# Turning the 128-row tiles by ScalarE copies and VectorE 32x32 block transposition instead of by TensorE, in a two-layer kernel on one core

## The reference, cut to what matters

```
# layer 0
y = conv1d(x, weight, groups=4, taps=9) + cond @ c_weight.T + bias      # (64, 64, 1024)
base = y @ base_w.T + base_b
top 2 of 16 experts by softmax(y @ router_w.T), combine weights
delta = sum_e combine[e] * (y @ A.T) @ B[e].T * 0.5                      # rank 64
x = x + base + delta
# layer 1
att = softmax(mlp(cond));  mixW = sum_k att[k] weight[k];  y = mixW @ x + att @ bias_k
top 2 of 28 experts by y @ gate_W.T
x = x + y @ base_W.T + sum_e gate[e] * 2 * (y @ lora_A[e].T) @ lora_B[e].T   # rank 8
```

## Time and profile before

| | |
|---|---|
| median of three runs | 1252.92 us (1252.64 to 1259.85) |
| the profiled execution | 1253.69 us |
| its span, first to last instruction | 1251.9 us |
| granted TensorE clock, mean | 0.997 |
| busy: TensorE, its weight loads | 1228.3 us (98%), 1093.2 us |
| busy: VectorE, ScalarE, GpSimd | 636.9, 376.2, 286.7 us |
| DMA | 266.94 MB, mean 213 GB/s |

### The profile page before, as it was taken

One profiled execution on the slowest core, in us unless ns is written; L12 is line 12 of the kernel. 1 busy time (PEld: TensorE's weight loads), 2 busy tenths in 40 slices (PEclk: granted clock), 3 DMA queues, 4 the chain that ended last, 5 costly groups with the idle time before them and its releaser, 6 DMA issues.

```text
span 1251.9 us, 21917 instructions
## 1 busy us (share of the span) xinstructions
PE 1228.3 (98%) x7263; PEld 1093.2 (87%) x7263; DVE 636.9 (51%) x1807; ACT 376.2 (30%) x801; POOL 286.7 (23%) x307
## 2 busy tenths in 40 slices
PE   6999989999999999999999999999999999999998
PEld 6999989999999999999888787887888888888887
DVE  6666466556555444547744343353345454354452
ACT  4312212212333334333343433434322212222221
POOL 2012543333222222225412121111121211211200
PEclk9999999999999999999999999999999999999999
DMA  7566656765899999988799999999864454445410
GB/s 285 186 221 222 229 189 224 246 229 211 240 298 292 309 308 296 320 279 215 178 246 283 281 267 288 283 274 285 247 140 118 98 118 116 92 118 110 103 50 34
DMA packets 85179, 266.94 MB, mean 213 GB/s; under 512 B 23457, under 2 KB 27937, under 8 KB 77858
## 3 DMA queue, kind: packets, MB, share of 16 engines
q1 hardware_dynamic: 72608, 230.12, 56.8%
q0 software_dynamic: 11264, 35.66, 16.1%
q10 hardware_dynamic: 1266, 0.70, 0.2%
HBM read 154.24 MB, written 112.20 MB: 213 GB/s over the span
## 4 chain that ended last, share of the span: by engine, by line
PE 85%; DMA 5%; DVE 3%; issue 2%; POOL 2%; SPq 2%; ACT 1%; ACTq 0%; POOLq 0%; DVEq 0%
PE z L1367 22%; PE z L1369 21%; PE z L1368 21%; DMA x8raw<-in_x_dram 3%; PE c L1367 3%; PE c L1369 3%; PE c L1368 3%; PE c L1432 2%; PE t L1488 2%; PE c L1434 2%; PE c L1436 2%; PE t L1408 2%; DMA x_dram<-xb 1%; SPq L434 1%; POOL hs_dram L665 1%
## 5 line engine op out<-in xcount | busy, mean ns | idle before, releaser
L1367 PE MATMUL z<-w_1h,yh 128*128 128x512 f32 (+1 forms) x504 | 187.4, 372 | 0.0
L1367 PE MATMUL z<-w_0h,yh 128*128 128x512 f32 (+1 forms) x504 | 186.0, 369 | 0.0
L987 DVE TENSOR_TENSOR yl<-t,yh 128x512 fp32r<-128x512 f32 x126 | 81.0, 685 | 205.6 <-ACT yh L743 205.5
L1369 PE MATMUL z<-w_1l,yh 128*128 128x512 f32 (+1 forms) x504 | 183.6, 364 | 0.0
L1369 PE MATMUL z<-w_0l,yh 128*128 128x512 f32 (+1 forms) x504 | 183.2, 364 | 0.0
L1368 PE MATMUL z<-w_1h,yl 128*128 128x512 f32 (+1 forms) x504 | 183.1, 363 | 0.0
L1368 PE MATMUL z<-w_0h,yl 128*128 128x512 f32 (+1 forms) x504 | 182.8, 363 | 0.0
L1367 PE MATMUL z<-w_2h,yh 128*128 128x252 f32 (+1 forms) x504 | 151.5, 301 | 8.6 <-DVE before L1045 5.0
L658 POOL TENSOR_TENSOR carrier<-ones_col 128x1 f32<-128x1 f32 x96 | 23.2, 242 | 576.7 <-DVE den L1054 139.3
L1369 PE MATMUL z<-w_2l,yh 128*128 128x252 f32 (+1 forms) x504 | 150.5, 299 | 0.0
L1368 PE MATMUL z<-w_2h,yl 128*128 128x252 f32 (+1 forms) x504 | 150.5, 299 | 0.0
(11 more groups left out here) (219 smaller groups left out, 2476.4 us busy)
## 6 DMA issues: line engine op xcount, KB each, us to landing
bd<-bd_dram SPq DMA_DIRECT2D x96, 512.0 KB, 6.6
zs_dram<-zt SPq DMA_DIRECT2D x96, 512.0 KB
hs_dram<-zt SPq DMA_DIRECT2D x34, 512.0 KB
x8raw<-in_x_dram SPq DMA_DIRECT2D x32, 516.0 KB
xin<-in_x_dram SPq DMA_DIRECT2D x32, 512.0 KB
x_dram<-xb SPq DMA_DIRECT2D x32, 512.0 KB, 7.8
out_dram<-xb SPq DMA_DIRECT2D x32, 512.0 KB, 2.9
bd_dram<-bd SPq DMA_DIRECT2D x8, 1024.0 KB
```

The lines of the kernel that those rows point to most:

```text
L987: V.tensor_tensor(o, v, y_places(s, high, b)[0], ALU.subtract).then_inc(s.y_lo[b], 1)
L1367: T.matmul(o, ah, wh, start=start, stop=False, **kw)
L1369: return T.matmul(o, ah, wl, start=False, stop=stop, **kw)
```

## The change: who turns the rows

For all tiles but tile 0 of layer 0 and tiles 0, 1 and 16 of layer 1 (there TensorE still turns), a tile is turned in two steps. `mid` holds the rows. ScalarE copies it to a new buffer `moved` in 16 copies of 32 partitions x 256 elements (`moves`, two parts of 8), each from one quadrant of 32 partitions to another, so that every 32x32 block already stands in the quadrant where it must end. Then VectorE transposes every 32x32 block within its quadrant, from `moved` back into `mid` (`turn_rows`: four instructions of 256 elements in layer 0, two of 512 in layer 1). `y_high` and `y_low` read `mid` in SBUF in place of `tp` in PSUM. The weights of layer 1 are laid out by the host in the matching order. There are two buffers `yh` now, but still one `yl`, so `y_low(t+1)` now waits for `base_done[1]` of tile t, in both layers.

The order moves with it. In layer 0, ScalarE does part 0 of the moves of tile t+1 ahead of the exponentials and part 1 behind `x8_high(t+2)` and `b_high`, ahead of `w1_high` and `y_high`; with lists, `outputs` 2 and 3 now come behind `y_high`. VectorE does `turn_rows` behind `x8_low`, `b_low`, `w1_low` and `listed_places`, then `y_low`, and `residual(1)` only behind that. TensorE's `conv(t+2)` now waits for the third output of the list step, and each `listed_pair(s, 0)` for the last output of the step before. In layer 1 `mixing(t+1)` comes right behind `over_y(2)`, the first listed pair behind `over_y(0)`, the second behind `over_y(1)`; ScalarE does `mixed_out`, the 16 copies, the outputs 0 and 1, `h1h`, then `x1_high(t+2)` (a tile earlier than before), `y_high`, outputs 2 and 3. Tiles 0 and 15 of layer 1 keep the old order (`late`). TensorE's loops now do two tiles per turn.

The core of the diff (helpers that only changed their arguments and the loop heads are left out):

```diff
-        yh = sb(ctx, "yh", [P, KC, P], F32R)
+        yh = [sb(ctx, f"yh{u}", [P, KC, P], F32R) for u in range(2)]
+        moved = sb(ctx, "moved", [P, L])
...
+        def turned_by_tensor(s, t):
+            return at(t, 0) or s is a1 and (at(t, 1) or at(t, NA))
+        def turned_rows(s, t, y, b):
+            if not turned_by_tensor(s, t):
+                return y[:, 4 * b:4 * b + 4, :], mid[:, HALF * b:HALF * (b + 1)].rearrange("p (k r) -> p k r", r=P)
...
+            def moves(s, t, part):
+                if part == 0:
+                    for b in range(2):
+                        act.wait_ge(s.c_out[b], t + 1)
+                    act.wait_ge(s.y_ps[1], t)
+                for q in (2 * part, 2 * part + 1):
+                    rows, w = slice(Q * q, Q * (q + 1)), slice(KC * Q * q, KC * Q * (q + 1))
+                    for i in range(P // Q):
+                        o = moved[Q * i:Q * (i + 1), w]
+                        if s is a0:
+                            mm = copy(o.rearrange("p (n m) -> p n m", m=Q),
+                                      mid[rows, :].rearrange("p (n m) -> p n m", m=NB)[:, :, Q * i:Q * (i + 1)])
+                        else:
+                            mm = copy(o, mid[rows, KC * Q * i:KC * Q * (i + 1)])
+                if part:
+                    mm.then_inc(moved_ready, 1)
...
+                if turned and not first:
+                    moves(a0, t + 1, 0)
                 exps(a0, t)
...
                 if exists(t + 2):
                     x8_high(t + 2)
...
+                if turned:
+                    moves(a0, t + 1, 1)
                 if w1_piece is not None:
                     w1_high(2, w1_pieces(2)[w1_piece:w1_piece + 1])
+                if turned:
+                    y_high(a0, t + 1, 1 - u)
                 if lists:
                     outputs(s, 2, cp, first=first_list)
                     outputs(s, 3, tp, first=first_list)
...
+            def turn_rows(s, tiles):
+                dve.wait_ge(moved_ready, tiles)
+                for b in range(2):
+                    if s is a0:
+                        for q in (2 * b, 2 * b + 1):
+                            w = slice(KC * Q * q, KC * Q * (q + 1))
+                            mm = V.transpose(mid[:, w].rearrange("p (j n c) -> p n j c", j=2, c=CI),
+                                             moved[:, w].rearrange("p (n j c) -> p n j c", j=2, c=CI))
+                    else:
+                        k = slice(4 * b, 4 * b + 4)
+                        mm = V.transpose(mid[:, :].rearrange("p (k q r) -> p q k r", k=KC, r=Q)[:, :, k, :],
+                                         moved[:, :].rearrange("p (q k c) -> p q k c", k=KC, c=Q)[:, :, k, :])
+                    mm.then_inc(s.y_ps[b], 1)
...
+                if exists(t + 1):
+                    turn_rows(a0, t + 1)
+                    dve.wait_ge(base_done[1], t + (0 if at(t, TILES - 2) else 1))
+                    y_low(a0, t + 1, 1 - u)
                 if not at(t, TILES - 2):
                     residual(i, u, 1)
-                if exists(t + 1):
-                    y_low(a0, t + 1)
...
-                    if lists:
-                        pe.wait_ge(zt_out, PER * s + 4)
-                    turn_conv(t + 1)
...
                 if exists(t + 2):
+                    if lists:
+                        pe.wait_ge(zt_out, PER * s + 3)
                     conv(t + 2)
...
+                if not late and not last:
+                    pe.wait_ge(zt_out, PER * s - 1 if lists else PER * WS if at(t, 1) else PER * WAVES * WS)
+                    mixing(t + 1)
...
+                    pe.wait_ge(a1.c_out[1], t + 2)
+                    pe.wait_ge(zt_out, PER * s)
+                    listed_pair(s, 0)
...
-        "w1": w1.reshape(KC, P, L + GC).transpose(1, 0, 2), "lb": lb.reshape(K1, 2, L),
+        "w1": w1.reshape(P // Q, KC, Q, L + GC).transpose(0, 2, 1, 3).reshape(P, KC, L + GC), "lb": lb.reshape(K1, 2, L),
```

More of the change, by code:

```diff
@@ L270, in build @@
         x1 = xin + [x1_2, x1_3]
+        listed += [zt[2][:, 2 * R0 * n:2 * R0 * (n + 1)].rearrange("p (k r) -> p k r", k=2) for n in range(HELD - 2)]
         id_zero, id_ready, iota_ready = sem("id_zero"), sem("id_ready"), sem("iota_ready")
@@ L384, in y_places @@
             return y[:, 4 * b:4 * b + 4, :], tp[b][:, :].rearrange("p (k r) -> p k r", r=P)
-        last_y = [bd[0][:, n, :].rearrange("p (k r) -> p k r", r=P) for n in range(2)]
-        def y_of(s, t):
-            return last_y if s is a0 and at(t, TILES - 1) else (yh, yl)
         def own_buffers(t):
@@ L856, in step0 @@
                     outputs(s, 1, tp, first=first_list)
+                if turned and first:
+                    moves(a0, t + 1, 0)
                 if exists(t + 2):
@@ L869, in step0 @@
                     outputs(s, 3, tp, first=first_list)
-                if exists(t + 1):
-                    for b in range(2):
-                        y_high(a0, t + 1, b)
                 if turn is not None:
@@ L905, in _, with next_rows, step1 @@
             y_high(a1, 0, 0)
-            y_high(a1, 0, 1)
             act.wait_ge(xb_ready, TILES)
-            def step1(i, v, first=False, last=False, lists=False, turn=None):
-                t = 4 * i + v
-                s = t - S1_LISTS + WS
+            def next_rows(t, i, v):
+                if t + 2 < TILES if isinstance(t, int) else True:
+                    act.wait_ge(a1.c_ps[1], t + 2)
+                    x1_high(t + 2, i + (v + 2) // 4, (v + 2) % 4)
+                    mix_high(t + 2)
+            def step1(i, v, first=False, last=False, late=False, before_late=False, lists=False, turn=None):
+                t, u = 4 * i + v, v % 2
+                s = t - S1_LISTS + WS
+                exps(a1, t)
+                if not last and not late:
+                    mixed_out(t + 1)
+                    for part in range(2):
+                        moves(a1, t + 1, part)
+                if late:
+                    act.wait_ge(a1.c_ps[1], t + 1)
+                    x1_high(t + 1, i + (v + 1) // 4, (v + 1) % 4)
+                    mix_high(t + 1)
                 if first:
-                    exps(a1, 0)
-                    x1_high(1, 0, 1)
-                    mix_high(1)
                     act.wait_ge(base_done[1], TILES)
@@ L921, in step1 @@
                         copy(lbh[:, k, :], lbraw[:, k, :]).then_inc(lb_hi, 1)
-                else:
-                    if not last:
-                        act.wait_ge(a1.c_ps[1], t + 1)
-                        x1_high(t + 1, i + (v + 1) // 4, (v + 1) % 4)
-                        mix_high(t + 1)
-                    exps(a1, t)
                 if lists:
@@ L1327, in step1 @@
                     listed_places(1)
-                if not last:
-                    y_low(a1, t + 1)
+                if late:
+                    y_low(a1, t + 1, 1 - u)
+                    next_mix(t)
+                    next_rows(t, v)
+                elif not last:
+                    if not before_late:
+                        next_rows(t, v)
+                    dve.wait_ge(base_done[1], TILES + t + 1)
+                    y_low(a1, t + 1, 1 - u)
                 if at(t, 0):
@@ L1602, in step1 @@
                     count_lists(1)
-                if tables:
-                    list_tables(1)
-                if lists:
-                    listed_pair(s, 0)
+                if not late and not last:
+                    pe.wait_ge(zt_out, PER * s - 1 if lists else PER * WS if at(t, 1) else PER * WAVES * WS)
+                    mixing(t + 1)
                 if first:
@@ L1624, in step1 @@
                     pe.wait_ge(a1.z_out[1], t)
-                over_y(1, w1h, w1l, pieces=w1_lo[1] if first else None, chunks=range(KC // 2))
-                if lists:
-                    pe.wait_ge(zt_out, PER * s + 3)
-                if not last:
-                    mixing(t + 1)
-                over_y(1, w1h, w1l, pieces=w1_lo[1] if first else None, chunks=range(KC // 2, KC))
-                if lists:
-                    pe.wait_ge(zt_out, PER * s + 4)
+                over_y(1, w1h, w1l, y, pieces=w1_lo[1] if first else None, chunks=range(KC // 2))
+                if late:
+                    pe.wait_ge(zt_out, PER * WS * (1 if first else WAVES))
+                    mixing(t + 1)
+                over_y(1, w1h, w1l, y, pieces=w1_lo[1] if first else None, chunks=range(KC // 2, KC)).then_inc(base_done[1], 1)
+                if lists:
+                    pe.wait_ge(zt_out, PER * s + 2)
+                    listed_pair(s, 1)
                 if first:
                     pe.wait_ge(lists_ready, 3)
-                if not last:
+                if late:
                     turn_mixed(t + 1)
```

252 lines of the change are left out of this document (147 added, 105 removed).

## The result

The changed kernel takes 1246.38 us (median of 6 runs, 1242.1 to 1250.04) against 1256.93 us of the kernel before, run beside it (6 runs, 1252.64 to 1259.85): a ratio of 0.9921 [0.9892, 0.9949], a gain of some 10 us where 31 were forecast. Its profiled execution takes 1247.44 us, with a span of 1245.6; that is 6.25 us under the profiled execution of the kernel before.

The account below looks back on a forecast made before the run. TensorE, busy 98% of the span, was taken to bound the kernel, with DMAs close behind in list tiles. From 1253.69 us, +2 - 6 - 0.9 - 9.6 - 16.8 = -31.3 gave 1222.4, stated as 1222 us; range 1202 to 1260.

Parts of the forecast that it names:

- Layer 0 without lists: Tiles 1 to 18 turned: a 7.2 us chain behind `x8_high` takes up TensorE's gain; sum 2 us slower.
- a loop through SyncE's queue: Layer 0 without lists: clears and GpSimd's addition hold SyncE's queue some 16 us a tile, untouched by the change.
- I take 0.33 us for each: ScalarE's 256-element copies: 0.33 us each, 5.3 a tile, 2.65 a part of eight; upper bound 3.3 a part.
- GpSimd's interference: `y_low` beside GpSimd's addition: costed at nothing, up to 1.2 us a tile if the two meet.
- Tiles 1 to 4 gain about 1 each: Early tiles of layer 0 without lists: about 1 us gained each, then lost again in the queue.
- Tile 31 gains its 0.93: its chain has free time: Last tile of layer 0: keeps TensorE's whole 0.93 us gain, since its chain has free time.
- Layer 0 with lists: 12 tiles: `conv` loses 0.2 to 0.3 us to the third output, DMA share 0.98; half the gain taken, 6 us.
- Layer 1: 12 list tiles gain 0.8 us each, 9.6 us; 17 turned tiles without lists gain 0.99 each, 16.8 us.
- three signs of being wrong: Copy between quadrants 0.45 us or more; TensorE waiting for `yl` in layer 1; `x1_high` waiting for gathers over 3 us.
- Rival 1: Whole kernel: TensorE's full 57.5 us arrive, 1196 us, needing the input of `x8_high` earlier; chance 0.12.
- Rival 2: DMAs bind with lists: 24 tiles keep their period, 15.6 us of the gain go, 1238 us; chance 0.22.
- Rival 3: Layer 0 chain: copies don't overlap (+0.65 us), block transposition slower (+0.6); 39 us over 30 tiles, 1261 us; chance 0.21.

Follow-up runs that it names:

- short copies: Changed kernel with 4 copies over 128 partitions in place of 16 over 32, without the quadrant exchange (rows wrong): 1234.32 us, ratio 0.9814.
- outputs first: As "both", with `outputs` 2 and 3 ahead of `y_high` in layer 0 with lists: 1227.19 us, ratio 0.9778.
- both: Changed kernel with tiles 1 and 31 of layer 0 turned by TensorE and layer 1's list tables computed early: 1229.92 us, ratio 0.9795.

## Why the prediction was off

The sign was right and so was the gain of a running tile, but the path at the ends of the stages wasn't: 10 us by the medians against 31. In the profiled executions it is 6.3 against 31.3. Of these 25 us, 7.7 are lost in tiles 0 to 17, 7.1 in tiles 30 and 31, 4.6 in the first two tiles of layer 1, 2.8 ahead of tile 0, 2.8 in the rest of layer 1. By its own steps:

**Layer 0 without lists: right for the running tiles.** The forecast was that the chain behind `x8_high` takes up TensorE's gain (+2; without tile 0, +3.4 measured, and up to +7 in other versions with the same order). In tile 12, one before that of the earlier trace rows, the chain can be read off:

```profile
248.96 1.07 ACT L752 ACTIVATE x8h<-x8raw 128x1032 fp32r<-128x1032 f32 x1 [2.60 <-DMA x8raw<-in_x_dram]
250.05 3.40 ACT L752 ACTIVATE moved<-mid 32x256 f32<-32x256 f32 x8
...
254.28 1.28 ACT L752 ACTIVATE yh<-mid 128x512 fp32r<-128x512 f32 x2 [0.84 <-DVE mid L1044]
```

The copy starts 8.9 us into its tile. From 248.96 to the next tile's start at 256.93 it is 7.97 us, where 7.2 was worked out; the 0.75 us are the copies. In tiles where the input comes earlier the distance is up to 10 us, so this chain binds in some tiles only. That they didn't slow the stage more, and that shorter ones don't speed it up, fits the prediction's other statement, that this stage is paced by a loop through SyncE's queue. The three runs (290.4 with short copies, 289.0 twice with TensorE) show that neither the length of the copies nor TensorE's turning sets it to more than 1 or 2 us; that it is SyncE's loop was argued and not isolated.

**"I take 0.33 us for each": wrong**, from too distant a row. Copies over 128 partitions do follow each other at 0.31 us; these follow at 0.43, 3.4 us for a part, just above the upper bound of 3.3. The Trainium skill ("VectorE: DVE Perf Modes", the section on the TRN2 errata) gives 224 cycles over the elements, an estimate of 0.40 us for a single copy of 256; the means of 415 and 407 ns agree with it, and it is the distance, not the duration, in which the two kinds differ. The block transposition was priced right: four of 256 take 1.42 us (1.5), and one of 512 lasts 0.691 (0.685 taken).

The groups of the block transpositions of 512 and of `y_low`, in the changed kernel:

```profile
L1048 DVE STREAM_TRANSPOSE mid<-moved 128x512 f32<-128x512 f32 x58 | 37.9, 691 | 130.9 <-ACT moved L752 130.9
...
L1035 DVE TENSOR_TENSOR yl<-mid,yh 128x512 fp32r<-128x512 f32 x118 | 76.5, 690 | 30.3 <-PE z L1456 27.6 <-ACT yh L752 0.5
```

`y_low` takes 690 ns in the mean (685 before): costing GpSimd's interference at nothing was right.

**"Tiles 1 to 4 gain about 1 each": the first step that failed.** It looked at tiles that are already running. The turning of tile 1, in tile 0, has no tile before it to hide the first part. Of the 6.3 us that tile 0 lost, some 3.3 are its price and 3 the clock at the start. Tile 1, at the start of which TensorE had waited 2.5 us, took 17.4 us and not 15.4, with a clock of 0.66 from 49 to 54. The 2.8 us ahead of tile 0 belong to no part of the change: the versions with the same code there start at 20.4 to 21.4 us.

**"Tile 31 gains its 0.93: its chain has free time": the largest failure.** The turning of tile 31 is done in tile 30, which has no convolution and no list work for TensorE. There the turning on other engines takes longer than TensorE has matmuls to do, and its first part also holds up the exponentials: TensorE waits 2.9 us for `rank` and 2.7 for the rows. It is +6.2 us for the two tiles in place of -0.9: 4.5 in tile 30 (17.6 against 13.1) and 1.5 (18.0 against 16.5) by the lower clock after the waits.

**Layer 0 with lists: the right cause, the right number by luck.** -6 forecast, -6 measured, but the 6 was half of the gain, taken for want of a better number, with the DMAs' share as one of its reasons. The cause named (the third output late for `conv`) is the one that "outputs first" removes, for another 3.5 us against the changed kernel (4.8 against "both"); the DMAs took nothing.

**Layer 1: the gain per tile right, one edit not costed.** 0.98 us with lists in an undisturbed tile (22.80 to 21.82) and 0.89 to 0.90 at the end, where 0.99 was taken: 14.3 us for the 16 tiles there in place of 15.8. The seventeenth of the forecast's tiles is tile 1. In tile 1 the tables moved behind new work, and SyncE's load of `ht` with them: 5 us of the two tiles' time (44.2 against 39.2 when they are early), a wait of 3.15 us and a slow stretch behind it. The prediction put nothing down for the tables' move: it has no term for what `list_tables(1)` is queued behind. Its three signs of being wrong didn't find any of this. The copies stayed under 0.45 us, TensorE waited for `yl` in layer 1 only ahead of its first tile, and `x1_high` waited for gathers by over 3 us twice (3.7 us each, tiles 5 and 6) without costing TensorE a wait. One list tile with a second `ht` wait took 24.67 us, the rest of the difference to -9.6.

**Rival 1** (the full 57.5 us) fell with layer 0, where TensorE's shorter tiles turned into waits. **Rival 2** (the DMAs keep the periods) fell: the periods shrank in both stages. What is left of it are single waits for `ht` and for gathered rows, in other tiles from version to version. **Rival 3** had the copies right (they don't overlap: 0.75 us a part, where it had 0.65) and the block transposition wrong (1.42 us for four, not 2.1), and the place was wrong: in running tiles most of the price is hidden, and it is paid where cover is missing.

What stays open: what sets the single waits in layer 1's lists, which differ between versions with the same code there; what decides whether a wait of some 3 us is followed by the lower clock; and what pace SyncE's loop would allow without its clears.

## What to carry to other kernels

A step moved off the full engine is cheap only where that engine has other work for as long as the new path takes: check the first tile, the last ones and every change of stage apart from the steady tile, and keep the old way there. List each operation that the new order pushes back (here the tables behind a load) with what waits for it. For a run of small copies, read the distance between copies of the same partition count, not the duration of one.

## What the runs showed of the hardware

- ScalarE's copies of 256 elements last about 0.41 us over 128 partitions as over 32, but follow each other at 0.31 us in the one case and at 0.43 in the other (two in 0.72 us, eight in 3.41); reading another quadrant than the one written changes nothing (3.41 and 3.39 us for eight). Whether it is the count of partitions or the change of the first partition from copy to copy wasn't tried.
- The 32x32 block transposition of fp32 on VectorE takes 0.41 us for 256 elements, four in 1.42, and 0.69 for 512: as fast as a subtraction of two SBUF operands of 512 (0.69).
- In the changed kernel, two waits of TensorE close together (2.9 and 2.7 us by its weight loads) and one of 3.15 us were each followed by 5 us at a mean granted clock of 0.66, 1.7 us of work lost. Waits of 2.82 us there and of 3.38 us in another version were followed by a clock of 1.00. So a wait of this length can cost half as much again, and doesn't always.
- Tile 0 of layer 0 has a mean granted clock of 1.00 in two of the twelve profiled executions and of 0.87 to 0.93 in the ten others, with TensorE's turning and with copies alike. That is up to 3.1 us in a tile of 20, so a stage near the start can't be compared by its time alone.
